# GpSimd in place of VectorE for the high parts of keys and queries, with some positions of the hand-made order moved

## What is computed

```python
x = x + 0.5 * _L0_ffn_ref(_layernorm(x), ...)      # one matmul, low-rank part folded in
x = x + _L0_attn_ref(_layernorm(x), ...)           # 16 heads of 8; q and k normalised; two softmax steps
x = x + 0.5 * _L0_ffn_ref(_layernorm(x), ...)
x = x + 0.5 * _L1_ffn_ref(_layernorm(x), ...)      # 8 experts, top 2, and a shared one
x = x + _L1_attn_ref(_layernorm(x), ...)           # 16 heads of 8, block mask, softmax
x = x + 0.5 * _L1_ffn_ref(_layernorm(x), ...)
...
# in _L0_attn_ref
state = q
for _ in range(STEPS):                             # 2
    sim = jnp.einsum('bqhd,bkhd->bqhk', state, k)
    att = jax.nn.softmax(BETA * sim, axis=-1)
    state = jnp.einsum('bqhk,bkhd->bqhd', att, v)
```

## Time and profile before

| | us |
|---|---|
| runs | 3434.24, 3441.23, 3446.66 |
| median | 3441.23 |
| the profiled execution | 3455.04 |
| its span | 3453.2 |
| PE busy in it | 3178.5 |
| DVE busy | 2358.3 |
| ACT busy | 2077.4 |
| POOL busy | 1267.3 |

### The profile page before, as it was taken

The page is one execution under the profiler, slowest core; times in us unless marked ns, Lnnn a source line. Parts: engine busy times, 40 slices in busy tenths (PEclk is TensorE's granted clock), DMA queues, the critical chain, the costliest instruction groups (busy, mean ns, idle before and its releaser), DMA issues.

```text
span 3453.2 us, 55298 instructions
## 1 busy us (share of the span) xinstructions
PE 3178.5 (92%) x19942; PEld 1655.9 (48%) x19942; DVE 2358.3 (68%) x5153; ACT 2077.4 (60%) x2689; POOL 1267.3 (37%) x2419
## 2 busy tenths in 40 slices
...
GB/s 42 1 32 3 33 1 8 28 32 35 32 35 29 32 17 23 35 32 35 29 32 16 24 35 32 35 30 32 35 5 35 32 35 31 30 32 4 60 35 35
DMA packets 81502, 96.89 MB, mean 28 GB/s; under 512 B 50544, under 2 KB 68400, under 8 KB 81104
## 3 DMA queue, kind: packets, MB, share of 16 engines
...
...
## 4 chain that ended last, share of the span: by engine, by line
PE 61%; ACT 15%; DVE 14%; POOL 5%; issue 4%; SPq 0%; DMA 0%; ACTq 0%; DVEq 0%; POOLq 0%
PE ps L689 16%; PE ps L706 14%; ACT probs L820 13%; PE ps L771 8%; PE ps L761 8%; DVE negmax L1072 6%; PE ps L589 5%; PE ps L726 4%; PE ps L595 2%; PE ps L584 2%; PE ps L654 1%; DVE hid L1141 1%; DVE uts L1039 1%; DVE th L1135 1%; DVE X L951 1%
## 5 line engine op out<-in xcount | busy, mean ns | idle before, releaser
L820 ACT ACTIVATE probs<-ps 128x1024 f32<-128x1024 f32 x1536 | 1573.6, 1024 | 1009.3 <-PE ps L689 994.3
L1072 DVE TENSOR_REDUCE negmax<-ps 128x2 f32<-128x1024 f32 x1024 | 1250.3, 1221 | 450.9 <-PE ps L726 432.8
L689 PE MATMUL ps<-qT,kT 32*128 32x512 f32 x3072 | 778.8, 502 | 116.7 <-ACT probs L820 68.7
L706 PE MATMUL ps<-probs,v 128*32 128x512 f32 x6144 | 838.5, 618 | 0.0
L1310 POOL TENSOR_TENSOR xe<-xT_m,G 128x512 f32<-128x512 f32 x288 | 367.7, 1278 | 990.7 <-PE ps L761 945.1
L761 PE MATMUL ps<-xe,w_sb 128*128 128x256 f32 x2304 | 655.3, 409 | 13.2 <-DVE hid L1141 8.9
L689 PEld LDWEIGHTS ps<-qT,kT 32*128 32x128 f32 x3072 | 289.0, 184 | 766.9 <-ACT probs L820 506.0
L726 PE MATMUL ps<-kT,qT 32*128 32x512 f32 x2048 | 520.5, 503 | 57.2 <-DVE negmax L1072 56.5
L761 PEld LDWEIGHTS ps<-xe,w_sb 128*128 128x128 f32 x2304 | 399.2, 192 | 185.5 <-issue 132.6
L1135 DVE SCALAR_TENSOR_TENSOR th<-th,ps 128x256 f32<-128x256 f32 x576 | 236.3, 411 | 187.5 <-ACT th L850 182.2
L850 ACT ACTIVATE th<-ps 128x256 f32<-128x256 f32 x576 | 221.0, 384 | 151.0 <-PE ps L761 138.5
...
## 6 DMA issues: line engine op xcount, KB each, us to landing
...
maxrow<-negmaxT SPq DMA_DIRECT2D x512, 2.0 KB
v<-v_tok SPq DMA_DIRECT2D x256, 18.0 KB, 1.9
...
```

The source lines that it names most:

```text
L689: nc.tensor.matmul(ps[:, B_ST + h, :], kT[a][rows, g * S + kc * P:g * S + (kc + 1) * P], qT[a][rows, g * S:(g + 1) * S], start=True, stop= ...
L706: ins = nc.tensor.matmul(ps[ROWS * j:ROWS * (j + 1), B_UT, :], v[:, at:at + ROWS], probs[:, n % QUADS, j, :], start=(kc == 0), stop=(kc == ...
L820: nc.scalar.activation(probs[:, quad % QUADS, j:j + 2, :], ps[:, B_ST:B_ST + 2, :], ACT.Exp).then_inc(sem["exp_done"], 1)
L1072: nc.vector.tensor_reduce(negative[:, tc, 2 * half:2 * half + 2], ps[:, B_SM:B_SM + 2, :], AX_X, ALU.max, negate=True).then_inc(sem["sm_re ...
```

## The change

Four things are different.

POOL makes the high parts. `low_parts` is now `parts`: a cast, a wait for that cast (`link`), and then the subtraction and the copy as before. DVE's `p0_hi` and `p1_hi` are gone, with their semaphores; POOL waits for what DVE waited for. There are 64 casts of 128x512 in all, four to a batch.

The lag of `uts` on DVE is 0.2 in place of 0.4, that of `ffn_rest` 0.8 in place of 1.0. The first S2 maximum job of a batch begins at 32 in place of 31 (not in the first two batches, which have tables of their own). `m_index` stands at least 1.4 behind `m_probs` in place of 0.9, and `m_pick` follows it. The other new names hold the numbers that stood there before.

```diff
-DIVIDE_AT, STATE_AT = 11.2, 12.9
+DIVIDE_AT, STATE_AT = (11.2, 11.2, 11.2, 11.2), (12.9, 12.9, 12.9, 12.9)
+FFN_XT, M_XT, P0_XT = 0.2, 0.2, 0.2
+FFN_AGGR, M_AGGR, P0_AGGR, P1_AGGR, PROBS, INDEX, PICK = 1.0, 1.0, 1.0, 1.0, 1.2, 1.4, 1.0
...
-S2_MAX_AT = (31, 42, 63, 73)
+S2_MAX_AT = (32, 42, 63, 73)
...
-            "m_gu": 1.6, "turn": 1.4, "p1_qkv": 0.8, "sm": 0.6, "uts": 0.4, "p0_qkv": 1.0, "ffn_y": 1.0, "ffn_rest": 1.0, "state": 0.0, "o_y": 0.8, "divide": 0.0, "mx": 0.0},
+            "m_gu": 1.6, "turn": 1.4, "p1_qkv": 0.8, "sm": 0.6, "uts": 0.2, "p0_qkv": 1.0, "ffn_y": 1.0, "ffn_rest": 0.8, "state": 0.0, "o_y": 0.8, "divide": 0.0, "mx": 0.0},
...
-    t.at(start + 6.6, "m_index", b, k, behind=(("m_probs", b, k), 0.9))
-    t.at(start + 6.6 + 1, "m_pick", b, k, behind=(("m_index", b, k), 1))
+    t.at(start + 6.6, "m_index", b, k, behind=(("m_probs", b, k), INDEX))
+    t.at(start + 6.6 + 1, "m_pick", b, k, behind=(("m_index", b, k), PICK))
...
-            def p0_hi(n, b, i):
-                dve.wait_ge(sem["p0_unit"], b + 1)
-                nc.vector.tensor_copy(heads0(i)[:, :, :, 0:HD].bitcast(F32R), source_of(0, i)).then_inc(sem["p0_hi"], 1)
...
-            def p1_hi(n, b, i):
-                if i == 0:
-                    dve.wait_ge(*read(("p1_qkv", b, TC - 1)))
-                nc.vector.tensor_copy(heads1(i)[:, :, :, 0:HD].bitcast(F32R), source_of(1, i)).then_inc(sem["p1_hi"], 1)
...
-            def low_parts(stacked, source, i, signal):
+            def parts(stacked, source, i, signal):
+                link(nc.gpsimd.tensor_copy(stacked[:, :, :, 0:HD].bitcast(F32R), source))
                 lo, dup = (HD, 2 * HD) if i == 0 else (2 * HD, HD)
                 nc.gpsimd.tensor_tensor(stacked[:, :, :, lo:lo + HD].bitcast(F32R), source, stacked[:, :, :, 0:HD],
                                         ALU.subtract)
                 nc.gpsimd.tensor_copy(stacked[:, :, :, dup:dup + HD], stacked[:, :, :, 0:HD]).then_inc(signal, 1)
...
             def p0_hi(n, b, i):
-                pool.wait_ge(sem["p0_hi"], n + 1)
-                low_parts(heads0(i), qk_heads(0, i), i, sem["p0_lo"])
+                pool.wait_ge(sem["p0_unit"], b + 1)
+                parts(heads0(i), qk_heads(0, i), i, sem["p0_lo"])
...
             def p1_hi(n, b, i):
-                pool.wait_ge(sem["p1_hi"], n + 1)
-                low_parts(heads1(i), qk_heads(1, i), i, sem["p1_lo"])
+                if i == 0:
+                    pool.wait_ge(*read(("p1_qkv", b, TC - 1)))
+                parts(heads1(i), qk_heads(1, i), i, sem["p1_lo"])
```

More of the change, by code:

```diff
@@ L225, in window @@
     if kind == "S1":
-        t.at(start + DIVIDE_AT, "divide", b, g)
-        t.at(start + STATE_AT, "state", b, g)
+        t.at(start + DIVIDE_AT[g], "divide", b, g)
+        t.at(start + STATE_AT[g], "state", b, g)
     else:
@@ L244, in ffn_events @@
     t.at(start, "ffn_stats", b, k, behind=(("o_y", b, 0), 1) if k else None)
-    t.at(start + 1, "ffn_aggr", b, k, behind=(("ffn_stats", b, k), 1))
-    t.at(start + 1.4, "ffn_xt", b, k, behind=(("ffn_stats", b, k), 0.2))
+    t.at(start + FFN_AGGR, "ffn_aggr", b, k, behind=(("ffn_stats", b, k), FFN_AGGR))
+    t.at(start + 1.4, "ffn_xt", b, k, behind=(("ffn_stats", b, k), FFN_XT if k else 0.2))
     t.at(start + 2.4, "ffn_bias", b, k, behind=(("ffn_xt", b, k), 0.8))
@@ L254, in moe_events @@
     t.at(start, "m_stats", b, k, behind=(("o_y", b, 1), 1) if k else (("ffn_y", b, 1), 2))
-    t.at(start + 1, "m_aggr", b, k, behind=(("m_stats", b, k), 1))
-    t.at(start + 1.4, "m_xt", b, k, behind=(("m_stats", b, k), 0.2))
+    t.at(start + M_AGGR, "m_aggr", b, k, behind=(("m_stats", b, k), M_AGGR))
+    t.at(start + 1.4, "m_xt", b, k, behind=(("m_stats", b, k), M_XT))
     t.at(start + 3.8, "m_logits", b, k, behind=(("m_xt", b, k), 1.8))
-    t.at(start + 5.2, "m_probs", b, k, behind=(("m_logits", b, k), 1.2))
-    t.at(start + 6.6, "m_index", b, k, behind=(("m_probs", b, k), 0.9))
-    t.at(start + 6.6 + 1, "m_pick", b, k, behind=(("m_index", b, k), 1))
+    t.at(start + 5.2, "m_probs", b, k, behind=(("m_logits", b, k), PROBS))
+    t.at(start + 6.6, "m_index", b, k, behind=(("m_probs", b, k), INDEX))
+    t.at(start + 6.6 + 1, "m_pick", b, k, behind=(("m_index", b, k), PICK))
     t.at(start + 9.2, "m_gt", b, k, behind=(("m_pick", b, k), 1.3))
@@ L288, in timeline @@
         t.at(p, "p0_stats", b, behind=(("ffn_y", b, 0), 2))
-        t.at(p + 1, "p0_aggr", b, behind=(("p0_stats", b), 1))
-        t.at(p + 1.4, "p0_xt", b, behind=(("p0_stats", b), 0.2))
+        t.at(p + P0_AGGR, "p0_aggr", b, behind=(("p0_stats", b), P0_AGGR))
+        t.at(p + 1.4, "p0_xt", b, behind=(("p0_stats", b), P0_XT))
         t.at(p + 4, "p0_res", b, behind=(("p0_xt", b), 1.4))
@@ L317, in timeline @@
         t.at(p, "p1_stats", b, behind=done)
-        t.at(p + 1, "p1_aggr", b, behind=(("p1_stats", b), 1))
+        t.at(p + P1_AGGR, "p1_aggr", b, behind=(("p1_stats", b), P1_AGGR))
         t.at(p + 1.4, "p1_xt", b, behind=(("p1_stats", b), 0.2))
@@ L443, in build @@
                                "ffn_var ffn_r ffn_biased ffn_done "
-                               "p0_var p0_r p0_res p0_squared p0_summed p0_unit p0_hi p0_lo "
-                               "p1_var p1_r p1_res p1_hi p1_lo v_moved "
+                               "p0_var p0_r p0_res p0_squared p0_summed p0_unit p0_lo "
+                               "p1_var p1_r p1_res p1_lo v_moved "
                                "zeroed prep m_var m_r m_shifted m_exped m_indexed m_gated m_ranked summed gates_out m_xe m_tanh m_gated_part")
```

11 lines of the change are left out of this document (2 added, 9 removed).

## The result

The changed kernel took 3462.89 us (median of 7 runs, 3458.34 to 3472.36), the kernel before 3441.23 us (7 runs, 3434.24 to 3448.86). The ratio is 1.006, with a 95% interval of 1.0043 to 1.0077. So it is slower, by 15 to 27 us. The profiled execution of the changed kernel took 3462.89 us, its span was 3461.1.

A forecast was written before the change was run, and what follows sets the result against it. PE was taken to set the end, busy 3178.5 of 3453.2 us, so only its waits count. The terms 9.1 - 8.4 + 4.8 + 6.0 + 2.4 = +13.9 us take the median from 3441.23 to 3455 us, range 3422 to 3480.

The forecast's parts named there:

- Term 1: Slot 87, PE waiting for POOL's copy: two casts ahead of it cost 0.7 us at each of 13 waits, +9.1 us.
- Rival E: POOL's cast is slow, 1.28 us like the subtraction: 3472 us; chance 0.08.
- Term 2: Slots 79 to 88, four casts fewer on DVE and layer 1's on POOL: 0, up to 0.5 us a turn.
- Term 3: Slot 14, `ffn_rest` ahead of a maximum: -8.4 us over twelve turns, bounds 0 and 13.7; slot 65: 0.
- Term 4: Slot 26, `uts` ahead of `m_up`: the next maximum begins 0.4 us later, +4.8 us for twelve turns, bounds 0 and 5.
- Term 5: Slots 41 to 43, S2 job one slot later: 0.5 us a turn, bounds 0 and 0.6, +6.0 us.
- Term 6: Slot 70, `m_pick` behind `m_gu`: POOL's gates come one DVE operation later, 0.2 us a turn is left, +2.4 us.
- Rival B: The moved DVE steps cost nothing and `ffn_rest` gives its whole 1.14 us: 3437 us, range 3429 to 3446; chance 0.29.
- rival D: Clock falls behind slot 87's longer wait in half of the turns, 3.1 us each, 19 us on top: 3474 us; chance 0.12.
- A: The forecast itself for the whole kernel: 3455 us, own range 3446 to 3464; chance 0.33.
- Rival C: A shorter wait at slot 14 and shifted turns end the lower clock, worth 23.8 us: 3422 us; chance 0.18.
- Its last sentence: Over all turns: the prediction is wrong in the whole if the turns' clock changes more than their waits do.

The follow-up runs named there:

- hi_early: The kernel before, casts on DVE, with both layer-0 subtractions and copies on POOL put ahead of the expert input and the addition of the maxima: 3437.21 us, ratio 0.9982.
- casts_l0: The kernel before with only layer 0's two casts on POOL, layer 1's still on DVE, nothing moved: 3469.71 us, ratio 1.0073.
- moves_only: The kernel before with the four moved positions, casts still on DVE: 3449.19 us, ratio 1.0020.

## Why the prediction was right, and where it wasn't

**Term 1, the casts on POOL's side: right in mechanism and size.** Cast 0.61, step 0.69, DVE's disturbance gone by 0.20 and 0.20. For the small operations 0.3 had been taken, and POOL's expert input of slot 85 does begin 0.3 earlier; slot 85 is 0.26 shorter. Forecast 0.7 for each of 13 waits, +9.1; measured 0.68 a turn in the slots, and in the waits of the changed kernel 6.8 for `stack0q` and ten times 0.2 for `stack0k`, +8.8. The wait for `stack0q` itself was forecast at 1.8 and is 1.61, since 0.19 came already in front of the keys. `hi_early` shows the same lever from the other side. Rival E, a slow cast, is out.

**Term 2, DVE's side at 0: right for the changed kernel.** Nothing moved in slots 79 to 84. But the reason given for layer 1, that its casts have slack, missed what `casts_l0` shows: on DVE they would have slowed POOL's new cast.

**Term 3, `ffn_rest`: right in kind, a little small.** Forecast -8.4; -0.83 a turn makes -10.0. At slots 14 to 17 it is -1.13 + 0.52, or -0.6 against the 0.7 forecast. At slots 66 to 69, where 0 was forecast, the move gains 0.23 (+0.48 and -0.71).

**Term 4, `uts`: the place was right, the size wrong.** Forecast +4.8. The slot behind 26 lost 0.29, as worked out, if less than 0.4. The failing step was the last: in slots 10 and 18 I took the move as worth 0, and behind slot 26 I let the delay stand for the whole turn. What was left out is that an earlier transpose also ends earlier: slot 11 gained 0.12 and slot 20 gained 0.16. Slot 51 lost 0.29, and slot 52 gave it back. The net is 0 a turn with slot 11 and +0.13 without it, so 0 to 1.6 us, and over the runs a gain that goes with the clock. The upper bound of 5 us was also short of the prediction's own words, which allowed another 0.4 a turn at slot 50.

**Term 5, the S2 job: right.** Forecast 0.5 at slots 42 and 43; measured 0.49, and 0.50 alone.

**Term 6, `m_pick`: too large.** Forecast 0.2 a turn; 0.11 alone and 0 in the changed kernel.

**The sum.** The schedule costs 6 to 7 us where the forecast had 13.9. Half of the forecast was missing, and what goes with the clock made up for it and more. That is luck and no merit of the sum. By the prediction's own sign terms 4 to 6 are wrong if turns at 1.00 are at 198.2 or below: `moves_only` has 198.10, where terms 3 to 6 gave 198.6. Rival B, that moved steps cost nothing, was right for terms 4 and 6 and wrong for term 5.

**The clock: rival D came true together with A.** D said that the clock would fall behind the longer wait at slot 87, in half of the turns, at 3.1 us each. It did so in 4 of 13 turns of the profiled execution, and for 3.4 us each, where the price of 3.1 us belongs to 6.8 us at the lower level. The direction and the place were right. What the prediction lacked is the second place, slot 67, where falls came with a move that was booked as a gain. Rival C had a share too: the falls at slots 11 to 14 are gone. It also treated A and D as alternatives, where they add. Its last sentence was the right warning: the turns' clock changed more than their waits did, by 7.8 against some 5.5 us in the eleven turns. Turns at 1.00 were forecast at 199.2; the changed kernel has none in batches 4 to 14, and by its slots one would take 198.7.
